# A decoder layer with int8-style quantisation: quantisation codes by token halves over three engines, and another order of transposes and cross attention

## Reference

```python
def _layernorm(x, eps=1e-05):
    m = mean(x, -1); v = var(x, -1)
    return (x - m) / sqrt(v + eps)

def xattn(ctx, x):             # linear attention, 16 heads of 8
    q = x @ Wq.T + bq; k = ctx @ Wk.T + bk; v = ctx @ Wv.T + bv
    att = (q per head) @ (k.T @ v per head) / sqrt(8)
    return layer_norm(att + x) * gamma + beta

def _affine_quantize(x):
    amin, amax = (jnp.min(x), jnp.max(x))
    scale = jnp.maximum((amax - amin) / 255.0, 1e-08)
    zp = jnp.clip(jnp.round(-amin / scale) + QMIN, QMIN, QMAX)
    q = jnp.clip(jnp.round(x / scale) + zp, QMIN, QMAX)
    return (q, scale, zp)

def _qlinear(x, W, b):
    xq, sx, zx = _affine_quantize(x)
    wq, sw = _sym_quantize(W)
    acc = jnp.einsum('bsh,oh->bso', xq - zx, wq)
    return acc * (sx * sw) + b

x1 = _layernorm(x + self_attention(x))
x2 = _layernorm(x1 + xattn(ctx, x1))
h  = gelu(_qlinear(x2, W1, b1))
y  = _layernorm(x2 + _qlinear(h, W2, b2))
```

## Time and profile before

| what | before |
|---|---|
| median of 3 runs | 468.15 us (468.12 to 468.48) |
| the profiled execution | 468.85 us, span 467.1 us |
| VectorE busy | 406.2 us, 87% |
| ScalarE busy | 346.7 us, 74% |
| TensorE busy (matmuls) | 238.0 us, 51% |
| GpSimd busy | 145.5 us, 31% |
| mean granted TensorE clock | 0.699 of full |

### The profile page before, as it was taken

One profiled execution on the slowest core, in us unless ns is written; L12 is line 12 of the kernel. 1 busy time (PEld: TensorE's weight loads), 2 busy tenths in 40 slices (PEclk: granted clock), 3 DMA queues, 4 the chain that ended last, 5 costly groups with the idle time before them and its releaser, 6 DMA issues.

```text
span 467.1 us, 6743 instructions
## 1 busy us (share of the span) xinstructions
PE 238.0 (51%) x1534; PEld 101.2 (22%) x1541; DVE 406.2 (87%) x1293; ACT 346.7 (74%) x789; POOL 145.5 (31%) x321
## 2 busy tenths in 40 slices
PE   1588864878577733333333333049995818115031
PEld 0553311323221210000000000013342716011031
DVE  3969997989699999999999999867977986977967
ACT  3679884979899955999999999926776655428133
POOL 2400000001000001999999999960000006420010
PEclk9999997999655555555555555559999766557557
DMA  7600000000344521699899998790003000000002
GB/s 265 158 1 1 0 1 1 22 22 25 135 180 180 200 94 67 146 202 201 200 201 200 203 202 180 135 224 3 1 1 125 29 0 1 1 0 0 0 0 92
DMA packets 84215, 43.21 MB, mean 92 GB/s; under 512 B 69063, under 2 KB 74455, under 8 KB 84058
## 3 DMA queue, kind: packets, MB, share of 16 engines
q1 hardware_dynamic: 82618, 42.69, 35.8%
q10 hardware_dynamic: 1568, 0.21, 0.3%
HBM read 7.75 MB, written 1.58 MB: 20 GB/s over the span
## 4 chain that ended last, share of the span: by engine, by line
DVE 34%; ACT 27%; PE 19%; issue 16%; ACTq 2%; DMA 1%; DVEq 0%
ACT mem L948 20%; PE ps L471 17%; DVE mem L1070 5%; DVE mem L1228 5%; DVE d_max L1073 3%; DVE mem L1491 2%; ACT mem L882 2%; DVE m L1628 2%; DVE m L1629 2%; ACT mem L918 2%; DMA gbc<-in_L_attn_ln_beta 1%; ACTq L948 1%; DVE c L1069 1%; DVE mem L1279 1%; DVE mem L1498 1%
## 5 line engine op out<-in xcount | busy, mean ns | idle before, releaser
L471 PE MATMUL ps<-mem 64*128 64x256 bf16 (+5 forms) x1182 | 180.5, 353 | 117.7 <-DVE row_max L1320 80.1
L948 ACT ACTIVATE mem<-mem,neg_max 128x256 f32<-128x256 int16 x256 | 125.8, 492 | 9.2 <-DVE neg_max L1069 9.2
L471 PEld LDWEIGHTS ps<-mem 64*128 64x128 bf16 (+3 forms) x1188 | 65.9, 119 | 224.6 <-DVE row_max L1320 108.7
L1320 DVE CUSTOM_DVE_ANT_0 mem<-ps,fold,c 128x256 int16<-128x256 f32 x256 | 110.9, 471 | 0.2 <-DVE fold L1070 0.2
L429 POOL TENSOR_SCALAR mem<-mem,r_now 128x256 int16<-128x256 f32 x176 | 81.6, 485 | 76.5 <-DVE r_now L1069 76.3
L1228 DVE TENSOR_TENSOR mem<-mem 128x1024 bf16<-128x1024 bf16 x76 | 49.6, 686 | 5.6 <-ACT mem L882 2.9
L898 ACT ACTIVATE mem<-ps,c 128x1024 bf16<-128x1024 f32 x48 | 48.4, 1295 | 1.5 <-PE ps L471 1.5
L948 ACT ACTIVATION_READ_ACCUMULATOR mem<-mem,neg_max x256 | 47.5, 185 | 0.0
L918 ACT ACTIVATE mem<-ps,c 128x1024 int16<-128x1024 f32 x32 | 36.4, 1211 | 12.7 <-DVEq L1263 7.4
L1073 DVE TENSOR_REDUCE d_max<-ps 128x1 f32<-128x1024 f32 (+1 forms) x34 | 37.9, 1125 | 3.0 <-PE ps L471 3.0
L429 POOL TENSOR_SCALAR bv_fine<-mem,r_now 128x256 int16<-128x256 f32 x80 | 36.8, 482 | 2.3 <-DVE r_now L1069 2.2
(11 more groups left out here) (203 smaller groups left out, 362.5 us busy)
## 6 DMA issues: line engine op xcount, KB each, us to landing
mem<-mem SPq DMA_DIRECT2D x64, 256.0 KB, 2.3
mem<-in_L_attn_w_qkv SPq DMA_DIRECT2D x1, 1536.0 KB, 9.6
mem<-in_x SPq DMA_DIRECT2D x2, 512.0 KB, 5.4
mem<-in_x SPq DMA_DIRECT2D x1, 1024.0 KB, 5.5
out<-mem SPq DMA_DIRECT2D x4, 256.0 KB, 2.2
xattn_matrix<-mem SPq DMA_DIRECT2D x1, 512.0 KB
mem<-in_L_attn_w_out SPq DMA_DIRECT2D x1, 512.0 KB, 4.8
mem<-in_L_ffn_W SPq DMA_DIRECT2D x2, 256.0 KB, 5.1
```

What stands on the lines that cost most here:

```text
L471: return te.matmul(o_, l_, r_, start=start, stop=stop)
L948: ins = sc.activation(e_ring[:, u % 4, pos], y_ring[:, u % 4, pos], ACT.Exp, scale=scale_reg, bias=neg_max[:, u % 4, pos:pos + 1], accum_o ...
L1320: ins = ve.tensor_tensor_reduce(y_ring[:, slot, pos], ps[:, 2 * slot + pos // 2, (pos % 2) * N:(pos % 2 + 1) * N], shift, col("g_dots"), - ...
```

## The change

Three things are edited.

1. TensorE's order in cross attention: transposes of quarters 0 and 1, then attention of quarter 0, transposes 2, attention 1, transposes 3, attention 2, attention 3.
2. Codes of x2: ScalarE makes the int16 values of both halves as soon as the inverse scale is there; VectorE makes the zero point meanwhile (split off from `affine` as `zero_point`) and then only clips. VectorE copies both transposed halves. The eight GELU units come in the order of `HID_UNITS`: two feature blocks of the first token half, the same of the second, then the other two blocks.
3. Codes of the hidden values: every integer and clip instruction works on 1024 tokens instead of 2048. VectorE starts its first block's first half before the zero point. All codes of the first token half come first, then those of the second. TensorE starts the first 8 tiles when the first half's four clips are done.

```diff
+        HID_UNITS = [(2 * k + j, h) for k in range(HC // 2) for h in range(2) for j in range(2)]
...
             pool.wait_ge(sem("hid_inv"), 1)
-            pl.tensor_scalar(hid_i[:, 2], hid[:, 2], col("inv"), 0.0, ALU.mult, ALU.add)\
-                .then_inc(sem("hid_i_pool"), 1)
+            for h in range(2):
+                cols = slice(h * UNIT, (h + 1) * UNIT)
+                pl.tensor_scalar(hid_i[:, 2, cols], hid[:, 2, cols], col("inv"), 0.0, ALU.mult, ALU.add)\
+                    .then_inc(sem("hid_i_pool"), 1)
...
             pe.wait_ge(sem("xm_again"), 32)
-            for q in range(3):
+            transpose_x1(0)
+            for q in range(1, 4):
                 transpose_x1(q)
-            for q in range(3):
-                cross_attention(q)
-            transpose_x1(3)
+                cross_attention(q - 1)
             cross_attention(3)
...
-            for u in range(2 * HC):
-                hc, h = u // 2, u % 2
-                if u < 2:
-                    pe.wait_ge(sem("x2T_act" if h else "x2T_dve"), 1)
+            for u, (hc, h) in enumerate(HID_UNITS):
+                pe.wait_ge(sem("x2T"), h + 1)
...
-            pe.wait_ge(sem("hid_codes"), HC)
             for t in range(TILES):
+                pe.wait_ge(sem("hid_codes"), HC * (1 + t // 8))
...
-            act.wait_ge(sem("x2T_ps"), 2)
-            sc.activation(x2T[:, UNIT:], ps[:, 7].bitcast(BF16), ACT.Copy).then_inc(sem("x2T_act"), 1)
+            act.wait_ge(sem("x2_inv"), 1)
+            for h in range(2):
+                sc.activation(x2_i[:, 8 * h:8 * h + 8], x2[:, 8 * h:8 * h + 8], ACT.Copy,
+                              scale=col("inv")).then_inc(sem("x2_i"), 1)
...
-            for hc in (1, 3):
-                sc.activation(hid_i[:, hc], hid[:, hc], ACT.Copy, scale=col("inv")).then_inc(sem("hid_i_act"), 1)
+            for h in range(2):
+                for hc in (1, 3):
+                    cols = slice(h * UNIT, (h + 1) * UNIT)
+                    sc.activation(hid_i[:, hc, cols], hid[:, hc, cols], ACT.Copy, scale=col("inv"))\
+                        .then_inc(sem("hid_i_act"), 1)
...
                 dve.wait_ge(sem(name + "_inv"), 1)
+
+            def zero_point():
+
                 link(ts(gb_i[:, 0:1], x2c[:, 1:2], col("inv"), None, ALU.mult))
...
             affine("x2", m2, 4, col("s_x2"))
+            zero_point()
             ts(col("s_x2w1"), col("s_x2"), s2w[:, 0:1], None, ALU.mult)
             for h in range(2):
                 half = slice(8 * h, 8 * h + 8)
-                link(ts(x2_i[:, half], x2[:, half], col("inv"), col("lo"), ALU.mult, ALU.max))
-                ts(x2_c[:, half], x2_i[:, half], col("hi"), None, ALU.min).then_inc(sem("x2_codes"), 1)
-            dve.wait_ge(sem("x2T_ps"), 1)
-            ve.tensor_copy(x2T[:, 0:UNIT], ps[:, 6].bitcast(BF16)).then_inc(sem("x2T_dve"), 1)
+                dve.wait_ge(sem("x2_i"), h + 1)
+                ts(x2_c[:, half], x2_i[:, half], col("lo"), col("hi"), ALU.max, ALU.min).then_inc(sem("x2_codes"), 1)
+            for h in range(2):
+                dve.wait_ge(sem("x2T_ps"), h + 1)
+                ve.tensor_copy(x2T[:, h * UNIT:(h + 1) * UNIT], ps[:, 6 + h].bitcast(BF16)).then_inc(sem("x2T"), 1)
...
             affine("hid", m2, 4, col("s_hid"))
+
+            def hid_first(h):
+                cols = slice(h * UNIT, (h + 1) * UNIT)
+                ts(hid_i[:, 0, cols], hid[:, 0, cols], col("inv"), None, ALU.mult).then_inc(sem("hid_i"), 1)
+
+            def hid_codes(h):
+                cols = slice(h * UNIT, (h + 1) * UNIT)
+                for hc in (0, 2, 1, 3):
+                    if hc == 0:
+                        dve.wait_ge(sem("hid_i"), h + 1)
+                    elif hc == 2:
+                        dve.wait_ge(sem("hid_i_pool"), h + 1)
+                    else:
+                        dve.wait_ge(sem("hid_i_act"), 2 * h + 1 + hc // 2)
+                    ts(hid_c[:, hc, cols], hid_i[:, hc, cols], col("lo"), col("hi"), ALU.max, ALU.min)\
+                        .then_inc(sem("hid_codes"), 1)
+
+            hid_first(0)
+            zero_point()
             ts(col("s_hw2"), col("s_hid"), s2w[:, 1:2], None, ALU.mult)
-
-            link(ts(hid_i[:, 0], hid[:, 0], col("inv"), None, ALU.mult))
-            for hc in (0, 1, 2, 3):
...
-                ts(hid_c[:, hc], hid_i[:, hc], col("lo"), col("hi"), ALU.max, ALU.min).then_inc(sem("hid_codes"), 1)
+            hid_codes(0)
+            hid_first(1)
+            hid_codes(1)
```

More of the change, by code:

```diff
@@ L1620, in _ @@
                 half = slice(8 * h, 8 * h + 8)
-                link(ts(x2_i[:, half], x2[:, half], col("inv"), col("lo"), ALU.mult, ALU.max))
-                ts(x2_c[:, half], x2_i[:, half], col("hi"), None, ALU.min).then_inc(sem("x2_codes"), 1)
-            dve.wait_ge(sem("x2T_ps"), 1)
-            ve.tensor_copy(x2T[:, 0:UNIT], ps[:, 6].bitcast(BF16)).then_inc(sem("x2T_dve"), 1)
+                dve.wait_ge(sem("x2_i"), h + 1)
[3 more added lines that the diff above has]
+                ve.tensor_copy(x2T[:, h * UNIT:(h + 1) * UNIT], ps[:, 6 + h].bitcast(BF16)).then_inc(sem("x2T"), 1)
             for u in range(2 * HC):
                 dve.wait_ge(sem("gelu_done"), u + 1)
-                part = hid[:, u // 2, (u % 2) * UNIT:(u % 2 + 1) * UNIT]
+                hc, h = HID_UNITS[u]
+                part = hid[:, hc, h * UNIT:(h + 1) * UNIT]
                 ve.tensor_reduce(m8[:, 0, u:u + 1], part, AX.X, ALU.max)
@@ L1632, in _ @@
             affine("hid", m2, 4, col("s_hid"))
-            ts(col("s_hw2"), col("s_hid"), s2w[:, 1:2], None, ALU.mult)
-            link(ts(hid_i[:, 0], hid[:, 0], col("inv"), None, ALU.mult))
-            for hc in (0, 1, 2, 3):
[L1637 to L1640, removed]
-                ts(hid_c[:, hc], hid_i[:, hc], col("lo"), col("hi"), ALU.max, ALU.min).then_inc(sem("hid_codes"), 1)
+            def hid_first(h):
[14 more added lines that the diff above has]
+            zero_point()
+            ts(col("s_hw2"), col("s_hid"), s2w[:, 1:2], None, ALU.mult)
+            hid_codes(0)
+            hid_first(1)
+            hid_codes(1)
             def output(q):
```

## The result

The changed kernel takes 466.62 us (median of 10 runs, 465.26 to 467.42), the kernel before 469.26 us in the same ten rounds. The ratio is 0.9945, with an interval from 0.9933 to 0.9958: 0.55% faster, about 2.6 us. The forecast was 467.1 us, or 1.06 us less than before; rival A was 2.2 us less. The forecast's 467.1 stood on the earlier median of 468.15 for the kernel before; from 469.26 the same difference would give 468.2.

What follows compares the result with a forecast made beforehand. VectorE, busy for 87% of the span, was taken to bound the kernel, with port waits shared with GpSimd. 1.27 - 0.87 - 1.46 = -1.06 us from the median of 468.15 gave 467.1 us, range 465.7 to 468.3.

Steps and rivals of the forecast that it cites:

- rival A: Cross attention: VectorE wins the port for sum3(0), so part 1 loses only 0.1 us; -2.2 us in all, 466.0; chance 33%.
- the end of X2: Cross attention: TensorE's attention of quarter 2 is ready for VectorE at 394.83 us instead of 394.36.
- the turn at sum3(0): Cross attention: GpSimd's product at 395.58 takes the shared port 0.06 us ahead of VectorE's sum at 395.64.
- I let it rise at 394.04 again: Cross attention: TensorE's granted clock goes from 0.50 to 0.98 at the same time as in the earlier profile.
- a T of 1.10 us: Cross attention: the transposes of one quarter cost TensorE 2.20 / 2 = 1.10 us.
- GpSimd's steps: Cross attention: additions hold the port until 391.04; products start at 392.68 for quarter 0 and 395.58 for quarter 1.
- the price of a lost turn: Cross attention: sum3(0) waits for GpSimd's product and ends at 397.40 instead of 396.13, 1.27 us lost.
- X0: Cross attention: attention of quarter 0, ready for VectorE one set of transposes earlier, at 388.4 us instead of 389.43.
- the place of the clips: Hidden codes: the clips wait for GpSimd's second half, then run from 448.05 to 449.97; TensorE starts at 450.01.
- My better bound, 1.8: Hidden codes: GpSimd's second half waits behind all four clips, half 0 is done at 449.0; 1.8 us won.
- rival B's case: Hidden codes: GpSimd takes both port turns before VectorE, part 3 wins only 0.3 us; 468.3, no change; chance 14%.
- The tail: From output(1) on: VectorE's own work, so output(1) coming at 453.72 instead of 455.18 gives the full 1.46 us.

Runs made afterwards that it cites:

- four more sets: Changed kernel with four extra repeats of quarter 3's transposes, delaying the attention of quarter 2; stretch from second transposes to zero point 33.82 us (changed kernel 32.16).
- the three parts alone: Kernel before with only one of the three edits each; ratios to before 0.9988 (part 1), 0.9994 (part 2), 0.9958 (part 3).
- three more sets: Changed kernel with three extra repeats of quarter 3's transposes; stretch from second transposes to zero point 32.57 us (changed kernel 32.16).
- kernels with more sets: Changed kernel with two, three or four extra repeats of quarter 3's transposes; stretch from second transposes to zero point 32.14, 32.57 and 33.82 us.

## Why the prediction was right, and where it was off

The direction was right, and the time fell in the range. The size was off by 1.5 us in the medians (1.06 us of gain forecast, 2.6 found) and by 2.0 in the profiles, where 1.7 of it come from part 1. What happened was rival A's case, in which VectorE wins the turn, and not the forecast's. That the measured 466.62 us lie within 0.5 us of the forecast's 467.1 is luck: the kernel before measured 1.1 us more in the new rounds than the median that the forecast stood on, and that made up for most of the missing gain.

- **Part 1: 1.27 us of loss forecast, 0.43 of gain found.** The step that failed is the end of X2, 10.19 us behind the second transposes, and with it the turn at sum3(0): X2 was ready near 8.7. Two of its terms were wrong. The first is "I let it rise at 394.04 again": the clock rose 2.9 us earlier relative to the work. I had taken the time of the rise from one execution as if it belonged to the kernel. The four profiles with the old order show 6.4, 6.6, 9.4 and 9.4. The Trainium skill says in "TensorE: Matmul & The Clock Gate", "Part 1: The HAM clock gate", that the point of the rise varies from run to run. These profiles agree, but the page's half a microsecond either way is far less than the 3.0 us measured here. The second term is a T of 1.10 us between two attentions. In the chain it is 0.85 (388.93), so even at the half clock X2 would start at 1.12 + 2.54 + 0.85 + 2.54 + 0.85 = 7.90 instead of 8.40. GpSimd's steps held (its product at 10.94), and the price of a lost turn was confirmed with four more sets. What gives the gain is the chain that I followed with the right sign: X0 and the shift of quarter 0 earlier, then GpSimd's product of quarter 0, at 393.31 - 385.27 = 8.04 instead of 393.09 - 384.64 = 8.45. Behind it come the shift of quarter 1 and GpSimd's addition, for which sum3(0) waits. In the changed kernel sum3(0) ends 396.34 - 385.27 = 11.07 us behind the transposes, before 396.13 - 384.64 = 11.49. Rival A, with the turn won, had 0.1 of loss and no gain, since I held it to X2's late time too.
- **Part 2: 0.87 forecast, 0.82 found**, with the copy costing nothing, as said.
- **Part 3: 1.46 forecast, 1.83 found.** The mis-sized term is the place of the clips. I let all four wait for GpSimd's second half (codes of half 0 at 450.0 - 445.3 = 4.7 us); the first clip got in ahead of it, and half 0 was coded at 4.3. My better bound, 1.8, has the right size but not the mechanism: it had GpSimd wait behind all four clips. A row of clips takes 1.92 / 4 = 0.48 each, as counted. Of what I held to be the risks of the part, who has the first turn hardly matters: in the kernel where GpSimd has it TensorE starts 0.06 us later. There VectorE still got in between GpSimd's halves, so rival B's case itself is not measured. Behind TensorE's start the 3.71 us to output(1) held, with the clock of that execution; with an earlier rise they were 3.43 and 3.61.
- **The tail** from output(1) on was VectorE's own, as said: output(2) came 2.50 us behind output(1) before and 2.49 after.

The three stages as measured add up to 3.08 us of gain. The times show 2.6, between 2.0 and 3.1 by the interval, and the ratios of the three parts alone multiply to 0.9940, or 2.8 us; all of these agree within their intervals.

Open is whether the new order ever meets the late clock, and what it costs then. An estimate from the rows above: X2 starts at 7.90, has done 1.50 of the forecast's 2.58 us when the clock rises at 9.40, and the rest takes half, so it is ready at 9.94. That is beside the kernel with three more sets (10.01, turn won, 32.57) and not the one with four (10.27, turn lost, 33.82). So a late clock would take back part 1's gain, but by this estimate, with 0.2 us to spare, not bring the forecast's loss. No profile shows it.

## What to carry to other kernels

A row that depends on the granted clock is one draw: look for the same work in another profile before a step rests on its time, and forecast both. Where two engines share a port, follow who asks first at each meeting; a quarter of a microsecond in front of the meeting (X2 at 10.01 or 10.27) cost a whole instruction, 1.25 us, behind it. And ask which engine a stage ends with before you give the busiest one a helper: GpSimd took 0.6 us off VectorE, and none of it reached the time, because the first half's codes came no earlier. Here ScalarE was the better helper: no clip waited at the port for it, and the first half was coded 0.49 us earlier.

## What the runs showed of the hardware

- A lead of 0.05 to 0.15 us decided the turn, either way: 0.05 for VectorE (first clip 0.54 us), 0.11 for VectorE (sum 0.67 us), 0.15 for GpSimd (sum 1.66 us).
- Neither engine kept the port from one of its instructions to the next when the other waited: the first clip (446.34) got in between GpSimd's halves, and GpSimd's second half between two clips that VectorE had in a row (446.34 and 446.79).
- VectorE's operations on one element per partition (zero point) ran at 0.14 to 0.22 us beside a GpSimd instruction, where the shift on four waited for it (0.54, 0.85 us). It isn't the four elements alone: a reciprocal of four took 0.18 us beside GpSimd's product (393.84).
- The granted clock rose 6.0 to 6.6 us or 9.4 us behind the same point, the second transposes; nothing between came up in 14 profiles.
- An attention took 2.54 us in the chain at a granted clock of 0.50 and 1.42 at 1.00 (kernels with more sets).
